# Four-layer attention and FFN chain on one core: in attention 1 and 2, VectorE writes the query's remainder ahead of the last two maxima and the shifts

## The reference

```python
def _L2_xattn_ref(query, key, value, mask, w_q, b_q, w_k, b_k, w_v, b_v, w_o, b_o):
    Q = _split_heads(query @ w_q.T + b_q)          # 16 heads x 8
    K = _split_heads(key @ w_k.T + b_k)
    V = _split_heads(value @ w_v.T + b_v)
    scores = jnp.einsum('bhqd,bhkd->bhqk', Q, K) * scale
    scores = jnp.where(mask, -jnp.inf, scores)
    attn = jnp.einsum('bhqk,bhkd->bhqd', jax.nn.softmax(scores, axis=-1), V)
    return merged @ w_o.T + b_o
# layer 1: the same without mask and without output projection
x = x + _L1_xattn_ref(_layernorm(x), ctx, ctx, ...);  x = x + _L1_ffn_ref(_layernorm(x), ...)
x = x + _L2_xattn_ref(_layernorm(x), ctx, ctx, mask, ...);  x = x + _L2_ffn_ref(_layernorm(x), ...)
```

## Time and profile before

| | us |
|---|---|
| median of 3 runs | 797.53 (795.21 to 801.01) |
| the profiled execution | 796.41, span 794.6 |
| TensorE busy | 542.4 |
| VectorE busy | 488.7 |
| ScalarE busy | 422.1 |
| GpSimd busy | 289.8 |
| maxima L1728, 160 of them | 103.8 |
| remainders L1744, 48 of them (16 of them in attention 3) | 16.8 |

### The profile page before, as it was taken

How to read it: one execution, slowest core, us unless ns; L and a number is a source line. 1 busy time by engine, 2 the same in 40 slices (tenths; PEclk the granted TensorE clock), 3 DMA queues, 4 the chain that set the end, 5 groups by cost and what they waited for, 6 DMA issues and landing times.

```text
span 794.6 us, 18439 instructions
## 1 busy us (share of the span) xinstructions
PE 542.4 (68%) x5614; PEld 362.4 (46%) x5619; DVE 488.7 (61%) x1420; ACT 422.1 (53%) x1029; POOL 289.8 (36%) x543
## 2 busy tenths in 40 slices
PE   5899999869997888884032233999994147881442
PEld 4677777655555645452011122556552125651231
DVE  2668787625444377776888954676766743326763
ACT  2757777744442266664276465555552024545774
POOL 2344455435654143321242255343412033424410
PEclk9989999978998599996555555799997558996555
DMA  8723333300000243330000002233320024540001
GB/s 236 213 57 76 80 69 66 77 13 1 0 11 16 60 110 97 104 86 10 1 0 0 0 1 60 71 98 82 89 71 11 0 69 127 144 129 0 0 1 53
DMA packets 102631, 47.54 MB, mean 60 GB/s; under 512 B 82160, under 2 KB 92080, under 8 KB 102448
## 3 DMA queue, kind: packets, MB, share of 16 engines
q1 hardware_dynamic: 102576, 46.87, 23.4%
HBM read 26.92 MB, written 19.92 MB: 59 GB/s over the span
## 4 chain that ended last, share of the span: by engine, by line
PE 28%; issue 25%; DVE 16%; POOL 8%; DMA 6%; ACT 5%; DVEq 5%; POOLq 3%; SPq 3%; ACTq 0%
DMA scratch_q<-q_parts 4%; PE bank L448 3%; PE bank L812 3%; PE bank L514 2%; PE bank L463 2%; DMA stacks<-scratch_q 2%; PE bank L785 2%; PE bank L787 2%; PE bank L555 2%; POOL tmp_a L1331 2%; DVE mx L1728 2%; PE bank L594 1%; PE bank L480 1%; DVE small L1538 1%; SPq L376 1%
## 5 line engine op out<-in xcount | busy, mean ns | idle before, releaser
L948 ACT ACTIVATE probs<-bank 128x512 f32<-128x512 f32 x160 | 90.9, 595 | 47.7 <-PE bank L484 44.6
L1728 DVE TENSOR_REDUCE mx<-bank 128x4 f32<-128x512 f32 x160 | 103.8, 683 | 19.5 <-PE bank L463 18.1
L1364 POOL CAST q_parts<-resid 128x128 bf16<-128x128 f32 x48 | 14.2, 295 | 96.5 <-DVE resid L1744 96.5
L514 PE MATMUL bank<-probs,v_slot 128*9 128x128 f32 x1024 | 45.1, 291 | 3.1 <-ACT probs L948 0.6
L1744 DVE SCALAR_TENSOR_TENSOR resid<-bank,w_bias_cols,q_parts 128x128 f32<-128x128 f32 x48 | 16.8, 350 | 49.0 <-ACT q_parts L998 49.0
L550 PE MATMUL bank<-w_ident,xn 128*128 128x128 f32 x64 | 21.8, 340 | 29.7 <-DVE xn L1704 18.0
L480 PE MATMUL bank<-stacks 48*128 48x128 bf16 x512 | 39.2, 227 | 3.2 <-DVE shift_t L1765 2.5
L484 PE MATMUL bank<-shift_t,pick_bf 64*128 64x128 bf16 x512 | 38.9, 225 | 0.0
L1021 ACT ACTIVATE att<-bank 128x512 f32<-128x512 f32 (+1 forms) x48 | 25.1, 522 | 21.9 <-PE bank L514 20.0
L705 PE MATMUL bank<-ident_bf,yq 128*128 128x128 bf16 x16 | 2.4, 306 | 47.3 <-DVE yq L1896 41.5
L1303 POOL TENSOR_TENSOR stats<-stats,half_neg 128x1 f32<-128x1 f32 x32 | 17.5, 546 | 46.7 <-DVE stats L1699 46.5
(11 more groups left out here) (304 smaller groups left out, 1707.4 us busy)
## 6 DMA issues: line engine op xcount, KB each, us to landing
stacks<-scratch_k SPq DMA_DIRECT2D x64, 96.0 KB, 2.2
stacks<-scratch_q SPq DMA_DIRECT2D x64, 96.0 KB, 2.2
scratch_k<-k_parts SPq DMA_DIRECT2D x48, 96.0 KB, 1.8
scratch_q<-q_parts SPq DMA_DIRECT2D x48, 96.0 KB, 1.9
scratch_k<-k_parts SPq DMA_DIRECT2D x48, 64.0 KB, 1.7
scratch_q<-q_parts SPq DMA_DIRECT2D x48, 64.0 KB, 1.7
stacks<-scratch_k SPq DMA_DIRECT2D x16, 192.0 KB, 2.6
stacks<-scratch_q SPq DMA_DIRECT2D x16, 192.0 KB, 2.5
```

The lines of the kernel that those rows point to most:

```text
L514: last = mm(bank[4][32 * j:32 * j + w, cols], v, probs[:, (s * U + u) % 4, j * T:(j + 1) * T], start=layer < 3, stop=True, skip_group_chec ...
L948: activation(probs[:, slot, :], bank[2 + u % 2][:, :], ACT.Tanh if layer == 3 else ACT.Exp, scale=float(d) ** -0.5).then_inc(sm["p"], 1)
L1728: top_ = reduce(mx[:, sM, at * UNIT:(at + 1) * UNIT], bank[u % 2][:, :].rearrange("p (h k) -> p h k", h=UNIT), AX.X, ALU.max)
```

## The change

In a step of attention 1 and 2, `q_rest` is issued ahead of the last two maxima and the shifts, and no longer behind them. Attention 0 and 3 are as before, and so are all other engines' lists.

```diff
--- before.py
+++ after.py
@@ -1854,10 +1854,10 @@
                         maximum(1)
                         statistics_ahead()
                         normalized()
+                        q_rest()
                         maximum(2)
                         maximum(3)
                         shifts()
-                        q_rest()
                         out()
                     else:
                         xn_ready()
```

## The result

| | before | after |
|---|---|---|
| median of 4 runs each, us | 796.60 (795.21 to 801.01) | 807.40 (802.17 to 815.35) |
| profiled execution, us (span) | 796.41 (794.6) | 802.17 (800.4) |
| attention 1, us | 90.39 | 96.30 |
| attention 2, us | 105.08 | 109.08 |

The ratio is 1.0095, 95% interval 1.0048 to 1.0141: slower by 3.8 to 11.2 us.

The account below looks back on a forecast made before the run. Attention 2 was taken as bound by TensorE, attention 1 by TensorE, VectorE and transfers in turn. Attention 1's +2.2 and attention 2's +3.75 us made +6 us, 803.5 us against the median of 797.5; range 796 to 810.

Parts of the forecast that it names:

- within 1%: Whole kernel: a median of 789.6 to 805.5 us, not told from no change; chance 0.68.
- item 5: Ordinary steps of attention 2: TensorE's value work covers the later shifts, cost 0; 1 us if cover were 0.2 us shorter.
- The third rival: First steps of turns: longer idle times bring the low clock, two more stretches up to 3 us, 806.5; chance 0.17.
- The forecast's own range: Whole kernel: 799 to 807 us around the forecast of 803.5, which had chance 0.53.
- items 1 and 2: Attention 1: ordinary steps pay +3.4 us on VectorE's loop; earlier stack transfers remove all waits, -4.9 us.
- The first rival: Attention 1: transfers decide and the wait for ScalarE is hidden, -4.9 us, 792.6; chance 0.13.
- item 3: Last step of a turn: next turn's statistics come 0.75 us later, three times, +2.25 us in each attention.
- item 4: Head, step 2 of each attention: uncovered wait for the query, 1.44 and 1.50 us, together +2.9 us.
- The prediction's sign of being wrong: Wrong if attention 1 shortens by more than 2 us, or TensorE in attention 2 waits for shifts in ordinary steps.

Follow-up runs that it names:

- the second measurement: The changed kernel measured again with no further edit, against the kernel before: 809.3 us, ratio 1.017 (1.012 to 1.022).
- head and last steps: Remainder moved only in steps 2, 3, 7, 11 and 15 of attention 1 and 2, against the kernel before: 808.4 us, ratio 1.015.
- the kernel that moves only the others: Remainder moved only in steps 4 to 6, 8 to 10, 12 to 14 of attention 1, against the kernel before: 797.9 us, ratio 1.002.
- The kernel without the head's moves: Remainder moved only in steps 7, 11 and 15 of both attentions, against the kernel before: 804.7 us, ratio 1.009.
- the written-out one: Steps written out for VectorE and GpSimd without branch, statistics always made ahead, remainder moved, against the kernel before: 793.1 us, ratio 0.991.
- the kernel before again: The kernel before, no edit, against itself: 797.2 us, ratio 0.998 (0.995 to 1.002).

## Why the prediction came out as it did

The forecast was 803.5 us, range 796 to 810, and "within 1%" the likeliest. The median of 807.4 and the ratio of 1.0095 lie inside, but at the upper end; the second measurement (809.3, ratio 1.017) is still inside the range but above 1%. The sum of 6 us was too low: profiles say 10 to 11 (below), the two ratios 7.6 and 13.5 us. But for item 5 the kinds of cost were right; that the first measurement fell within 1% is partly luck. The third rival, the lower clock, named 806.5; its share is real, but it is one of two causes. The forecast's own range was also wider than its terms: they give 800.6 and not 799 on the low side, and with the 1 us of item 5 804.5 and not 807 on the high side.

**The waits swap (items 1 and 2): right.** I had 3.4 - 4.9 = -1.5 us. In the profiles the nine ordinary intervals of attention 1 took 48.5 us before and 48.2 after, and steps 7 and 11 gained 0.8 us each from the earlier stack transfers (head and last steps, above): -1.9. Three executions with the old order in attention 1 have 47.8 to 49.6 us for the nine intervals, so their difference is within the scatter and only the sum is known to be small. The waits and the price are each confirmed: no wait for the stack is left, and an ordinary step without such a wait went from 4.95 to 4.98 us up to 5.39 to 5.47. What 4.9 us of waits are worth in time is less sure: without the remainder they fell by 3.8 us, and the intervals outside the first steps of a turn by 3.3. The first rival, that the shifts would be covered, falls with the same rows: TensorE waits for them in ten steps. The rule of the Trainium skill (DMA: Bandwidth & Descriptors, Rules for kernel authors) to issue a transfer early and wait for it late is borne out for the transfer, whose waits went from 4.9 us to none, and not for the time of the kernel, which is 1% longer.

**Last step of a turn (item 3): right in kind, too small.** I had 0.75 us three times per attention. Measured: 0.94 (step 3), 0.89 and 0.90 (steps 7 and 11, against the kernel that moves only the others) in attention 1, and 0.42, 1.11 and 1.04 in attention 2: 2.7 and 2.6 us instead of 2.25. I had taken the remainder's 0.35 us off the delay, since it no longer stood behind the shifts. But VectorE's own issue time at the branch, 0.45 us after the remainder, became 0.63 once the shifts stood directly ahead of it; about half of the 0.35 came back. Where the delay would be seen I had wrong: not as 2 us at the value copy, but as 1.09 at the turned scores (L480), and 0.88 at the mask products L448 in attention 2.

**The head (item 4): right.** 1.44 and 1.50 us were forecast; from the first maximum to the copy of step 3, 1.39 us were added in attention 1 and 0.99 in attention 2 (1.75 in the second execution; 1.5 on average over all), and TensorE's wait was 2.57 us, where I had said 2.6.

**Ordinary steps of attention 2 (item 5): the failed zero.** I had 0, with 1 us as a bound. The nine intervals went from 56.1 to 57.3 us, in small even amounts (6.25 and 6.29 became 6.39 and 6.49), and step 12, at full clock in both, from 7.04 to 7.17: with step 8 of the same kind and step 4, +1.9 us. The 0.09 us read off one row were a cover for the start of L569 only, not for the products behind it, which came 0.14 us later in the step shown. The prediction's sign of being wrong, "if TensorE in attention 2 waits for the shifts in ordinary steps", came true in the table of waits: the weight loads of L569 wait for them in ten more steps. The zero of item 5 was wrong, and the forecast held without it.

Without the first steps in which the clock differed, that is -1.9 + 5.3 + 2.4 + 1.9 = +7.7 us against a forecast of 6.

**The lower clock: a rival, not a remainder.** The rest of the 9.9 us are first steps of turns. For one such step, 12 of attention 1, the rows are, of the kernel changed in attention 2 alone (old code here), the changed kernel, and the changed kernel again:

```profile
330.52:337.50 6.98, 5.42 (x84) 3.61 (x86) 4.38 (x14) 4.19 (x10) 3.24 (x10) 0.76 0.34 87
```

```profile
326.59:333.63 7.04, 5.45 (x84) 3.51 (x86) 4.41 (x13) 4.21 (x10) 3.23 (x10) 0.76 0.27 72
```

```profile
330.27:337.97 7.70, 6.44 (x84) 4.31 (x86) 4.40 (x13) 4.36 (x10) 3.33 (x11) 0.57 0.26 65
```

Before, it was 6.24 us at 1.00. At 0.76 old and new code take the same time within 0.06 us; what differs is how much of the step falls into the lower of the two levels, 1.2 instead of 2.4 GHz. The mean clock alone does not fix the time: the kernel changed in attention 1 alone took 7.62 us for this step at 0.78. Step 4 of attention 1 is the one place where the change brings it each time: 0.99 to 1.00 and 5.55 to 5.56 us in all three executions with the old code in this attention, and in all three with the new one as here

```profile
276.56:283.99 7.43, 5.83 (x84) 3.78 (x86) 4.41 (x14) 4.36 (x10) 3.06 (x10) 0.77 0.27 70
```

or nearly so (7.38 at 0.77, 7.58 at 0.50): 1.9 us. Not all of this is the clock. TensorE is busy for 5.83 us of this step instead of 4.69, and idle for 1.60 instead of 0.87, so 1.1 us are slower products and 0.7 longer waits; the kernel with only the ordinary moves of attention 1 took 6.05 us for it at full clock. Adding these 0.5 to 0.7 us, what the change costs without the clock is 8.2 to 8.4 us, an estimate, and not 7.7. The other two kernels with the remainder moved in steps 2 and 3 have the low clock there too (7.12 at 0.76, 7.58 at 0.50). The kernel without the head's moves (5.56 at 0.92) and the written-out one (5.46 at 1.00) do not have it, so it takes the moves in steps 2 and 3 together with the turn's end behind step 3. Step 8 of attention 1 averages 7.80 with the new code and 6.93 with the old, three executions each. In attention 2 the clock decides step 8 whatever the order: of the changed kernel's two executions

```profile
536.85:544.02 7.17, 5.66 (x95) 3.48 (x95) 4.70 (x16) 4.48 (x11) 3.79 (x12) 1.00 0.27 71
```

```profile
542.17:551.77 9.60, 8.18 (x99) 4.92 (x99) 4.70 (x16) 4.42 (x11) 3.77 (x11) 0.66 0.23 61
```

one has it and one has not, as have the earlier trace rows and the kernel before again (7.05). These 2.4 us are nearly as much as item 3 costs in a whole attention. Averaged over the executions with old and with new code in an attention, it is 91.6 and 96.8 us in attention 1 (three each), 104.2 and 110.2 in attention 2 (five and three): +11 us. In these averages the first steps of a turn give 3.2 us in attention 1, but step 8 of attention 2 gives nothing (7.9 and 8.0 us): there the 6 us are the head, the last steps and the ordinary ones. I had bounded the clock by 3 us, which is about its size, and given it 0.17; the rows of one execution could show that it was possible, not how often.

**Open.** Why some first steps of a turn fall to the lower level and others of the same kernel do not is not settled. It also takes back gains: without the remainder, ordinary steps won 2.4 us, and steps 8 and 12 gave back 2.9 against the first execution, 2.0 against the mean of three. And the kernel with attention 2 alone lost 8.6 us by its ratio (4.8 to 12.4), of which its profile places 5: 109.15 us against 104.2.

## What to carry to other kernels

When a producer is moved ahead of its neighbours to release a transfer, price the whole list behind it: here 4.9 us of waits for a transfer went, and waits for the shifts behind the moved instruction came, in every kind of step. Look first at the steps that are not ordinary: 10 of the 28 moves, at the head and at the loop's end, cost as much as all 28 within what could be measured, and taking the irregular step away, by writing the loop out for two engines, brought 1.0% (0.7 to 1.3), where no place of the remainder brought anything. A cover read off one row is not a cover until the instructions behind the consumer have been read too: 0.09 us of it were worth nothing here.

## What the runs showed of the hardware

- At a loop's branch VectorE is idle for 0.45 to 0.48 us with the remainder ahead of it and for 0.63 to 0.66 with the shifts ahead of it (put down to its own issue ahead of L1695, each in at least two kernels).
- The granted clock of a same step of a same kernel differs between executions: 6.24 us at 1.00 and 7.84 at 0.57 for step 12 of attention 1, kernel before. In both, TensorE had waited 1.20 us at L594 within this step. From the end of attention 1 to the start of attention 2, where the kernel before has a mean granted clock of 0.52 and TensorE is busy for 41 of 133 us, all executions agree (133.7 to 134.2 us).
- The stretch ahead of attention 1, with equal instructions in all kernels but the one without the remainder, took 262.9 to 272.6 us, a spread of 1.2% of the whole.
